# Decoder kernel on one core: products made for other head pairs placed at other steps of a pair, and the doubled-key copies issued one and two steps later

## The chip, the cores and the metric

The kernel runs on one core of a Trainium2 chip. Its engines run their own instruction queues in order and wait for one another through semaphores: TensorE (PE, matrix products), VectorE (DVE), ScalarE (ACT), GpSimd (POOL), and SyncE (SP), which here issues nearly all DMAs. The metric is the device time in microseconds (us) of the whole program.

## The reference

Four batch rows of 1024 tokens of width 256 pass through six sublayers, each `x = x + f(layernorm(x))`: a kernel attention, a cross attention to 64 context rows, one expert of eight, a causal self attention with 16 heads of width 64, a second cross attention, and a gated feed-forward with quantised weights. The change lies in the self attention:

```python
q = jnp.einsum('bsd,hqd->bhsq', x, w_q)
k = jnp.einsum('bsd,hqd->bhsq', x, w_k)
v = jnp.einsum('bsd,hvd->bhsv', x, w_v)
scores = jnp.einsum('bhsq,bhtq->bhst', q, k)
masked = jnp.where(causal, -jnp.inf, scores)
weights = jax.nn.softmax(masked / jnp.sqrt(jnp.float32(dq)), axis=-1)
out = jnp.einsum('bhst,bhtv->bhsv', weights, v)
return jnp.einsum('bsf,df->bsd', cat, w_o)
```

## The kernel before

The four batch rows are done one after the other. In the self attention the 16 heads are 8 **pairs** j = 0 to 7, and a pair is 16 **blocks** k = 0 to 15: head 0, then head 1, each with its eight tiles of 128 query rows. The tiles come in the order 7, 0, 6, 1, 5, 2, 4, 3, and tile i has (i+1)*128 causal columns, so a block of even k is wide (1024, 896, 768, 640 columns) and one of odd k narrow (128 to 512). g = 16*j + k numbers the 128 blocks of a batch row. One block passes through these stations:

- PE `l_score`: scores into PSUM (lines 1271 to 1273, the last with `causal`). Wide blocks have two pairs of banks in turn, narrow ones all share bank 4.
- DVE `l_max`: row maximum `nmax` (line 1385). ACT `l_exp`: exponentials to `l_pb` (wide) or `l_ps` (narrow), line 1336. POOL: high half in f16 to `l_phb`/`l_phs` (line 1494). DVE `l_lower`: the remainder (line 1391), called the **remainder of block g** below.
- SP `l_flip`: one transposing DMA to `l_ptb`/`l_pts` (line 1503), called **flip g**. It waits for the remainder.
- PE `l_pv`: probabilities times values (line 1289), called **pv g**; it waits for flip g to land. DVE `l_finish` divides every fourth block (lines 1398, 1403).

All engines walk through the blocks in **steps** g in code order. At step g PE issues the scores of block g+6 (AHEAD = 6), then a task if the step has one, then pv g. ACT issues the exponential of block g+5 and then its part of the task. DVE issues the maximum of block g+6, its part of the task, the remainder of block g+4, and each fourth step a finish. SP issues flip g+4 and then copies or loads that are set for this step.

A **task** is a product made for another pair; `l_tasks(j, k)` says which task stands at which step. K0, K1, Q0, Q1 are the halves of the keys and queries of pair j+1 (6 matmuls of 512 columns, lines 233 to 235). V0 to V3 are the values for the next two pairs (in pairs 1, 3, 5). T0, T1 turn the output of pair j-1 (line 1225). O0 to O3 are the output projection of two done pairs (line 1250, in pairs 2, 4, 6). All tasks of the loop use PSUM bank 5, so `l_pe` makes a task wait until the bank's last reader of the task before it has run:

```python
before = in_bank5[in_bank5.index(t) - 1]
if before[0] == "T":
    pe.wait_ge(*upper(b, before))
else:
    pe.wait_ge(*lower(b, before))
```

"Upper" is ACT's part of a task (K: line 1347 into `xn`; Q: line 1351, two operations; T: line 1363), "lower" is DVE's, which waits for upper (K: line 1440, Q: line 1444, two operations each; O: line 1412 alone, without ACT). Pair 7 has tasks of its own (`CONTEXT`), which are not touched.

The keys are needed twice on 128 partitions. SP's `l_dup(j, h)` copies them for head h of pair j, two DMAs (line 1511), called **dup0** and **dup1**. `l_score` has the first block of a pair (k = 0, issued by PE at step 10 of the pair before) wait for the lower part of Q1 and for dup0, and block k = 8 for dup1:

```python
if i == NT - 1:
    pe.wait_ge(*lower(b, ("Q", j, 1)))
    pe.wait_ge(q_[f"dup{h}"], (b * HP + j + 1) * 32)
```

Of the kernel before, what the change touches and what calls it, by code (L numbers as in the profile page):

```python
# [19 lines left out]
HP = 8  # L20
# [37 lines left out]
def decoder_kernel(nc, a, out):  # L58
    ctx = ExitStack()
    with ctx:  # L60
# [1063 lines left out]
        q_ = l_sem  # L1124
# [11 lines left out]
        def l_tasks(j, k):  # L1136


            if j == HP - 1 and k in CONTEXT:
                return CONTEXT[k]  # L1140
            if k in (0, 1):
                return ("K", j + 1, k) if j + 1 < HP else None
            if k in (2, 3):
                return ("T", j - 1, k - 2) if j >= 1 else None
            if k in (4, 5):
                return ("Q", j + 1, k - 4) if j + 1 < HP else None
            if k in (7, 9, 11, 13):
                if j % 2 == 0 and j >= 2:
                    return "O", j // 2 - 1, (k - 7) // 2
                if j % 2 == 1 and j + 1 < HP:  # L1150
                    return "V", (j + 1) // 2, (k - 7) // 2
            return None

        FIRST_BANK = {("K", 0, 0): 2, ("K", 0, 1): 3, ("Q", 0, 0): 4, ("Q", 0, 1): 7,
# [10 lines left out]
        def made(b, t):  # L1165
            return q_["made"], b * len(N_MADE) + N_MADE[t]
# [4 lines left out]
        def lower(b, t):  # L1171
            return q_["lower"], b * len(N_LOWER) + N_LOWER[t]
# [233 lines left out]
        def l_make_lower(v, b, t):  # L1406
# [7 lines left out]
            if kind == "C":  # L1414
                v.wait_ge(*made(b, t))
                for c in range(2):
                    v.tensor_scalar(X1["c_kT"][:, c, :], bank[:, c * CK:(c + 1) * CK], x1_bk[:, c:c + 1], None, ALU.add)
                    v.tensor_scalar(X1["c_vT"][:, c, :], bank[:, (2 + c) * CK:(3 + c) * CK], x1_bv[:, c:c + 1], None, ALU.add)
                v.drain()
                for src, dst in ((X1["c_kT"], l_kC), (X1["c_vT"], X1["c_vC"])):  # L1420
                    for c in range(2):
                        last = v.tensor_tensor(dst[:, c, :].rearrange("p (h k) -> p h k", k=CK), src[:, c, :].unsqueeze(1).to_broadcast([P, 8, CK]),
                                               blk1[:].unsqueeze(2).to_broadcast([P, 8, CK]), ALU.mult)
                last.then_inc(q_["lower"], 1)
                return
# [96 lines left out]
        def l_sp(sp, b):  # L1522
            sp.wait_ge(s_xu, b * (NPH * NT) + 2 * NT)
            for j in range(2):
                l_load_w(sp, b, j)
            l_load_wv(sp, b, 0)
            l_load_wo(sp, b, 0)
            for h in range(2):
                l_dup(sp, b, 0, h)
            for g in range(4):  # L1530
                l_flip(sp, b, g)
            for g in range(NB):
                j, k = g // NB1, g % NB1
                if g + 4 < NB:
                    l_flip(sp, b, g + 4)
                if j + 1 < HP and k == 4:
                    l_dup(sp, b, j + 1, 0)
                if j + 1 < HP and k == 10:
                    l_dup(sp, b, j + 1, 1)
                if j + 2 < HP and k == 2:  # L1540
                    sp.wait_ge(*lower(b, ("Q", j + 1 - 1, 1)))
                    l_load_w(sp, b, j + 2)
                if j % 2 == 0 and j + 2 < HP and k == 2:
                    sp.wait_ge(*lower(b, ("V", j // 2, 3)))
                    l_load_wv(sp, b, j // 2 + 1)
                if j % 2 == 1 and j >= 3 and k == 2:
                    sp.wait_ge(*lower(b, ("O", j // 2 - 1, 3)))
                    l_load_wo(sp, b, j // 2)
# [549 lines left out]
```

## Time and profile before

| | |
|---|---|
| median of 3 runs | 3018.18 us (3016.68 to 3021.74) |
| the profiled execution, its own time | 3010.78 us |
| span of its trace | 3008.8 us |
| mean granted TensorE clock | 0.867 of full speed |
| busy: PE / DVE / ACT / POOL | 2276.8 / 2175.1 / 1060.2 / 585.9 us |
| self attention, four times | about 340, 335, 338 and 335 us |

The span is the part of the profiled execution between its first and last instruction. An engine's busy time counts neither its waits nor, for SP, the issuing of DMAs; a share under 100% in a stretch is time in which the engine waited for another. In a timeline, "[x <-E n]" behind a row is the idle time before it and what ended that idle time.

### The profile page before, as it was taken

The numbers are of one execution on the slowest core, as the hardware profiler recorded it, in microseconds if no ns is written. First come the engines' busy times: TensorE is split into PE (matmuls) and PEld (weight loads), VectorE is DVE, ScalarE is ACT, GpSimd is POOL, SyncE is SP. The second block draws the span as 40 slices with busy tenths as digits, with TensorE's granted clock in tenths as the row PEclk, the third lists the DMA queues.
The fourth block names the chain that finished last, engine by engine and source line by source line (L and its number), as shares of the span: only waits on it lengthen the run. The fifth ranks groups of instructions, "written<-read, shape, count | busy, mean of one in ns | idle before, by whom it ended". The sixth has DMA issues, their size and how long they took to land.

```text
span 3008.8 us, 50636 instructions
## 1 busy us (share of the span) xinstructions
PE 2276.8 (76%) x17470; PEld 1830.6 (61%) x17470; DVE 2175.1 (72%) x4246; ACT 1060.2 (35%) x2004; POOL 585.9 (19%) x666
## 2 busy tenths in 40 slices
PE   3667788868776877886877687888677777888875
PEld 3556666657465756664755565666565566666663
DVE  6765788866866578885776667888586666788767
ACT  2312444422432244442242224444224223444324
POOL 2111222212101122221101112222120102222220
PEclk8778899989777889998877789999877878999988
DMA  6001689840001078983000119897100014899600
GB/s 234 1 15 40 137 160 171 154 86 1 1 15 56 15 149 161 170 152 63 1 1 15 56 37 167 166 164 144 31 1 15 1 55 85 161 169 166 113 1 14
DMA packets 658407, 251.39 MB, mean 84 GB/s; under 512 B 613082, under 2 KB 633946, under 8 KB 657370
## 3 DMA queue, kind: packets, MB, share of 16 engines
q1 hardware_dynamic: 653978, 243.79, 41.4%
q10 hardware_dynamic: 4160, 4.19, 0.4%
q8 instruction: 146, 2.39, 0.3%
q14 instruction: 123, 1.01, 0.1%
HBM read 52.87 MB, written 10.49 MB: 21 GB/s over the span
## 4 chain that ended last, share of the span: by engine, by line
issue 38%; PE 23%; DVE 18%; DMA 11%; ACT 5%; POOL 4%; DVEq 1%; ACTq 0%; SPq 0%; POOLq 0%
DMA l_ptb<-l_phb 6%; PE ps L233 5%; PE ps L235 5%; PE ps L234 4%; DMA l_pts<-l_phs 4%; DVE nmax L1385 3%; PE ps L1289 1%; DVE l_k L1440 1%; DVE l_q L1444 1%; DVE l_phb L1391 1%; DVE l_phs L1391 1%; ACT l_q L1351 1%; PE ps L1271 1%; ACT xn L1347 1%; POOL d_pn L990 1%
## 5 line engine op out<-in xcount | busy, mean ns | idle before, releaser
L1385 DVE TENSOR_REDUCE nmax<-ps 128x1 f32<-128x1024 f32 (+7 forms) x512 | 383.3, 750 | 23.0 <-PE ps L1273 20.9
L1494 POOL CAST l_phb<-l_pb 128x1024 f16<-128x1024 f32 (+3 forms) x256 | 241.4, 943 | 654.1 <-ACT l_pb L1336 337.8
L1336 ACT ACTIVATE l_pb<-ps,nmax 128x1024 f32<-128x1024 f32 (+3 forms) x256 | 244.7, 956 | 283.5 <-DVE nmax L1385 282.7
L1271 PE MATMUL ps<-l_k,l_q 128*128 128x512 f32 (+3 forms) x768 | 319.1, 416 | 24.3 <-ACT l_ps L1336 23.9
L1391 DVE TENSOR_TENSOR l_phb<-l_pb,l_phb 128x1024 f16<-128x1024 f32 (+3 forms) x256 | 288.2, 1126 | 15.5 <-POOL l_phb L1494 13.4
L1272 PE MATMUL ps<-l_k,l_q 128*128 128x512 f32 (+3 forms) x768 | 270.1, 363 | 0.0
L1289 PE MATMUL ps<-l_v,l_ptb 128*128 128x64 f16 x4992 | 197.8, 197 | 34.2 <-DMA l_ptb<-l_phb 34.1
L1289 PEld LDWEIGHTS ps<-l_v,l_ptb 128*128 128x128 f16 x4992 | 177.1, 101 | 67.4 <-DMA l_ptb<-l_phb 41.1
L233 PE MATMUL ps<-xTh,l_w 128*128 128x512 f32 x256 | 123.1, 481 | 83.9 <-DVE l_q L1444 50.5
L1494 POOL CAST l_phs<-l_ps 128x128 f16<-128x128 f32 (+3 forms) x256 | 124.2, 485 | 319.1 <-DMA l_pts<-l_phs 169.6
L1271 PEld LDWEIGHTS ps<-l_k,l_q 128*128 128x128 f32 x768 | 156.0, 203 | 44.2 <-ACT l_ps L1336 29.8
L1336 ACT ACTIVATE l_ps<-ps,nmax 128x128 f32<-128x128 f32 (+3 forms) x256 | 135.5, 529 | 107.6 <-DVE nmax L1385 106.4
L1272 PEld LDWEIGHTS ps<-l_k,l_q 128*128 128x128 f32 x768 | 157.1, 205 | 12.6
L1289 PE MATMUL ps<-l_v,l_pts 128*128 128x64 f16 x1920 | 105.6, 200 | 62.1 <-DMA l_pts<-l_phs 61.8
L1391 DVE TENSOR_TENSOR l_phs<-l_ps,l_phs 128x128 f16<-128x128 f32 (+3 forms) x256 | 134.3, 525 | 25.1 <-POOL l_phs L1494 23.1
L303 PE MATMUL ps<-idf,xn 128*128 128x128 f32 x320 | 66.0, 374 | 108.0 <-DVE xTl L322 68.0
L1289 PEld LDWEIGHTS ps<-l_v,l_pts 128*128 128x128 f16 x1920 | 84.1, 102 | 104.1 <-DMA l_pts<-l_phs 68.7
L316 ACT CAST xTh<-ps 128x512 fp32r<-128x512 f32 x80 | 45.5, 587 | 285.7 <-PE ps L303 285.7
L985 POOL TENSOR_TENSOR x<-x,x_bo 128x2048 f32<-128x2048 f32 x8 | 36.2, 4521 | 553.7 <-DVE xn L284 553.7
L1440 DVE TENSOR_TENSOR l_k<-ps,xn 64x512 fp32r<-64x512 f32 x128 | 88.1, 689 | 73.1 <-ACT xn L1347 71.4
L1444 DVE SCALAR_TENSOR_TENSOR l_q<-ps,l_q 64x512 fp32r<-64x512 f32 x128 | 88.2, 689 | 68.8 <-ACT l_q L1351 66.6
L303 PEld LDWEIGHTS ps<-idf,xn 128*128 128x128 f32 x320 | 53.1, 195 | 117.9 <-DVE xTl L322 55.5
(361 smaller groups left out, 6279.4 us busy)
## 6 DMA issues: line engine op xcount, KB each, us to landing
l_k<-xn SPq DMA_DIRECT2D x128, 256.0 KB, 4.1
l_w<-l_wqk_s SPq DMA_DIRECT2D x32, 512.0 KB, 4.8
l_wv<-l_wv_s SPq DMA_DIRECT2D x16, 512.0 KB, 6.0
xin<-in_x SPq DMA_DIRECT2D x4, 1024.0 KB, 5.5
m_w<-in_m_w SPq DMA_DIRECT2D x8, 512.0 KB, 4.4
m_w<-in_m_w SPq DMA_DIRECT2D x4, 1024.0 KB, 9.2
l_wo<-in_l_wo SPq DMA_DIRECT2D x16, 256.0 KB, 4.5
l_ptb<-l_phb SPq DMA_TRANSPOSE x256, 4.1
```

Of the source, the lines that this page charges most:

```text
L233: pe.matmul(o, lh, rh, start=start, stop=False)
L234: pe.matmul(o, lh, rl, start=False, stop=False)
L235: return pe.matmul(o, ll, rh, start=False, stop=stop)
L303: last = pe.transpose(o, xn[:, tile, c * P:(c + 1) * P], idf[:])
L1271: pe.matmul(s[:, c0:c1], q, L["l_k1"][:, h, c0:c1], start=True, stop=False)
L1272: pe.matmul(s[:, c0:c1], q, L["l_k2"][:, j % 2, h, c0:c1], start=False, stop=c1 < n)
L1289: last = pe.matmul(o, l_turned(k)[:, pp * (i + 1) + m, :], L["l_v"][:, (j // 2) % 2, vv, m, cols], start=m == 0 and n == 0, stop=m == i an ...
L1336: s.activation(l_numer(k)[:, 0:n], l_banks(k)[:, 0:n], ACT.Exp, bias=nmax[:, k % 4:k % 4 + 1], accum_out=lsum[:, h, k % NT:k % NT + 1]).th ...
L1385: v.tensor_reduce(nmax[:, k % 4:k % 4 + 1], l_banks(k)[:, 0:n], AX.X, ALU.max, negate=True).then_inc(q_["max"], 1)
L1391: v.tensor_tensor(l_parts(k)[:, n:2 * n], l_numer(k)[:, 0:n], l_parts(k)[:, 0:n], ALU.subtract).then_inc(q_["lo"], 1)
L1444: last = v.scalar_tensor_tensor(out=L["l_q"][other, n % 2, h, halves(g)], in0=bank[mine, :], scalar=0.125, in1=f32(L["l_q"][mine, n % 2, h ...
L1494: g.tensor_copy(l_parts(k)[:, 0:cols], l_numer(k)[:, 0:cols]).then_inc(q_["hi"], 1)
```

## The change

Within a pair, K1 goes from step 1 to 4, Q0 and Q1 from 4 and 5 to 6 and 8, and V0 to V3 or O0 to O3 from steps 7, 9, 11, 13 to 10, 12, 14, 15. K0 (step 0) and T0, T1 (steps 2, 3) stay. SP issues dup0 at step 6 for 4 and dup1 at step 11 for 10. In pair 7 the lower part of the task C gets a wait for the last dup1, since it writes over the buffer that the copy reads.

```diff
-            if k in (0, 1):
-                return ("K", j + 1, k) if j + 1 < HP else None
+            if k in (0, 4):
+                return ("K", j + 1, k // 4) if j + 1 < HP else None
             if k in (2, 3):
                 return ("T", j - 1, k - 2) if j >= 1 else None
-            if k in (4, 5):
-                return ("Q", j + 1, k - 4) if j + 1 < HP else None
-            if k in (7, 9, 11, 13):
+            if k in (6, 8):
+                return ("Q", j + 1, k // 2 - 3) if j + 1 < HP else None
+            if k in (10, 12, 14, 15):
                 if j % 2 == 0 and j >= 2:
-                    return "O", j // 2 - 1, (k - 7) // 2
+                    return "O", j // 2 - 1, (10, 12, 14, 15).index(k)
                 if j % 2 == 1 and j + 1 < HP:
-                    return "V", (j + 1) // 2, (k - 7) // 2
+                    return "V", (j + 1) // 2, (10, 12, 14, 15).index(k)
...
                 v.drain()
+                v.wait_ge(q_["dup1"], (b * HP + HP) * 32)
...
-                if j + 1 < HP and k == 4:
+                if j + 1 < HP and k == 6:
                     l_dup(sp, b, j + 1, 0)
-                if j + 1 < HP and k == 10:
+                if j + 1 < HP and k == 11:
                     l_dup(sp, b, j + 1, 1)
```

Three places show what this does to the queues. First SP in pair 1, from flip 8 on (`128x16x128` is a flip of 1024 columns in two halves; `l_k<-xn` is half a dup). Before:

```order
L1503 DMA_TRANSPOSE l_ptb<-l_phb 128x16x128 [waits l_pv,l_lo]
L1511 DMA l_k<-xn 64x1024 [waits l_score,l_upper]
L1511 DMA l_k<-xn 64x1024
L1503 DMA_TRANSPOSE l_pts<-l_phs 128x2x128 [waits l_pv,l_lo]
L1503 DMA_TRANSPOSE l_ptb<-l_phb 128x14x128 [waits l_pv,l_lo]
L1503 DMA_TRANSPOSE l_pts<-l_phs 128x4x128 [waits l_pv,l_lo]
L1503 DMA_TRANSPOSE l_ptb<-l_phb 128x12x128 [waits l_pv,l_lo]
L1503 DMA_TRANSPOSE l_pts<-l_phs 128x6x128 [waits l_pv,l_lo]
L1503 DMA_TRANSPOSE l_ptb<-l_phb 128x10x128 [waits l_pv,l_lo]
L1511 DMA l_k<-xn 64x1024 [waits l_score,l_upper]
L1511 DMA l_k<-xn 64x1024
L1503 DMA_TRANSPOSE l_pts<-l_phs 128x8x128 [waits l_pv,l_lo]
```

After:

```order
L1504 DMA_TRANSPOSE l_ptb<-l_phb 128x16x128 [waits l_pv,l_lo]
L1504 DMA_TRANSPOSE l_pts<-l_phs 128x2x128 [waits l_pv,l_lo]
L1504 DMA_TRANSPOSE l_ptb<-l_phb 128x14x128 [waits l_pv,l_lo]
L1512 DMA l_k<-xn 64x1024 [waits l_score,l_upper]
L1512 DMA l_k<-xn 64x1024
L1504 DMA_TRANSPOSE l_pts<-l_phs 128x4x128 [waits l_pv,l_lo]
L1504 DMA_TRANSPOSE l_ptb<-l_phb 128x12x128 [waits l_pv,l_lo]
L1504 DMA_TRANSPOSE l_pts<-l_phs 128x6x128 [waits l_pv,l_lo]
L1504 DMA_TRANSPOSE l_ptb<-l_phb 128x10x128 [waits l_pv,l_lo]
L1504 DMA_TRANSPOSE l_pts<-l_phs 128x8x128 [waits l_pv,l_lo]
L1512 DMA l_k<-xn 64x1024 [waits l_score,l_upper]
L1512 DMA l_k<-xn 64x1024
```

Dup0 stood right behind flip 8 and now stands behind flips 9 and 10; dup1 stood between flips 14 and 15 and now stands behind flip 15.

Second DVE in pair 2, steps 4 to 6: from the finish of step 4 (line 1403) to the remainder of block 10 (`l_phb` 128x896), on which flip 10 waits. `nmax` rows are maxima. Before:

```order
L1399 REGISTER_ALU
L1402 REGISTER_ALU [waits l_pv,l_rc]
L1403 TENSOR_TENSOR xn<-ps,recs 128x4x64 [waits l_made]
L1384 REGISTER_ALU
L1385 TENSOR_REDUCE nmax<-ps 128x1 [waits l_score]
L1426 REGISTER_ALU
L1444 SCALAR_TENSOR_TENSOR l_q<-ps,l_q 64x512 [waits l_upper]
L1444 SCALAR_TENSOR_TENSOR l_q<-ps,l_q 64x512
L1391 TENSOR_TENSOR l_phs<-l_ps,l_phs 128x128 [waits l_hi]
L1384 REGISTER_ALU
L1385 TENSOR_REDUCE nmax<-ps 128x1 [waits l_score]
L1391 TENSOR_TENSOR l_phb<-l_pb,l_phb 128x896 [waits l_hi]
```

After (line numbers behind the added line are one higher):

```order
L1399 REGISTER_ALU
L1402 REGISTER_ALU [waits l_pv,l_rc]
L1403 TENSOR_TENSOR xn<-ps,recs 128x4x64 [waits l_made]
L1384 REGISTER_ALU
L1385 TENSOR_REDUCE nmax<-ps 128x1 [waits l_score]
L1391 TENSOR_TENSOR l_phs<-l_ps,l_phs 128x128 [waits l_hi]
L1384 REGISTER_ALU
L1385 TENSOR_REDUCE nmax<-ps 128x1 [waits l_score]
L1427 REGISTER_ALU
L1445 SCALAR_TENSOR_TENSOR l_q<-ps,l_q 64x512 [waits l_upper]
L1445 SCALAR_TENSOR_TENSOR l_q<-ps,l_q 64x512
L1391 TENSOR_TENSOR l_phb<-l_pb,l_phb 128x896 [waits l_hi]
```

The lower part of a query task now stands right ahead of the remainder of block 10, with both maxima ahead of it. Just above each piece stands the task of step 4, Q0 before and K1 after.

Third PE in pair 2, up to the first score of pair 3 (step 10). Before, from the scores of block 15 (step 9) on:

```order
L1263 REGISTER_ALU
L1271 MATMUL ps<-l_k,l_q 128x512 [waits l_exp]
L1272 MATMUL ps<-l_k,l_q 128x512
L1273 MATMUL ps<-causal,idb 128x128
L1308 REGISTER_ALU
L1250 MATMUL ps<-l_wo,xin 128x256 [waits l_lower]
L1250 MATMUL ps<-l_wo,xin 128x256 x3
L1289 MATMUL ps<-l_v,l_pts 128x64 [waits l_pt1]
L1289 MATMUL ps<-l_v,l_pts 128x64 x2
L1259 ISA [waits l_lower]
L1261 REGISTER_ALU [waits l_dup0]
L1271 MATMUL ps<-l_k,l_q 128x512 [waits l_exp]
```

After, from pv 8 on (the six matmuls of Q1 stand right above):

```order
L1282 ISA [waits l_o]
L1289 MATMUL ps<-l_v,l_ptb 128x64 [waits l_pt0]
L1289 MATMUL ps<-l_v,l_ptb 128x64 x23
L1263 REGISTER_ALU
L1271 MATMUL ps<-l_k,l_q 128x512 [waits l_exp]
L1272 MATMUL ps<-l_k,l_q 128x512
L1273 MATMUL ps<-causal,idb 128x128
L1289 MATMUL ps<-l_v,l_pts 128x64 [waits l_pt1]
L1289 MATMUL ps<-l_v,l_pts 128x64 x2
L1258 REGISTER_ALU
L1259 ISA [waits l_lower]
L1261 REGISTER_ALU [waits l_dup0]
```

The two waits, `l_lower` for Q1 and `l_dup0`, stand in the same place. Between Q1 and them stood the scores of blocks 12 to 15, pv 5 to 9 and two O tasks; now there are pv 8, the scores of block 15 and pv 9.

## Rows read from the trace of the kernel before

**Rows 1.** The page's first part: busy us of each engine.
```profile
PE 2276.8 (76%) x17470; PEld 1830.6 (61%) x17470; DVE 2175.1 (72%) x4246; ACT 1060.2 (35%) x2004; POOL 585.9 (19%) x666
```

**Rows 2.** Windows: the four self attentions summed (length, busy PE, PEld, DVE, ACT, POOL).
```profile
sum 1348.00, PE 1081.19 PEld 852.26 DVE 1074.87 ACT 601.26 POOL 359.47; mean PE 270.30 PEld 213.06 DVE 268.72 ACT 150.32 POOL 89.87
```

**Rows 3.** Waits of PE over the span: us in total, times, longest.
```profile
PE ps L1289 <- DMA l_pts<-l_phs: 61.8, 38, 3.9
PE ps L233 <- DVE l_q L1444: 50.9, 31, 1.9
PE ps L1289 <- DMA l_ptb<-l_phb: 34.1, 48, 1.9
...
PE ps L1225 <- DVE l_k L1440: 23.7, 24, 1.2
...
PE ps L233 <- DVE l_k L1440: 16.9, 22, 0.9
```

**Rows 4.** Timeline of PE, pair 4 of the last batch row: start, us.
```profile
2689.75 0.23 PE L1273 MATMUL ps<-causal,idb 128*128 128x128 bf16 x1
...
2697.29 0.66 PE L1225 MATMUL ps<-idf,xn 128*128 128x128 f32 x4 [0.93 <-DVE l_k L1440]
...
2700.85 0.50 PE L233 MATMUL ps<-xTh,l_w 128*128 128x512 f32 x1 [0.38 <-ACT xin L1363]
...
2705.23 0.50 PE L233 MATMUL ps<-xTh,l_w 128*128 128x512 f32 x1 [1.78 <-DVE l_q L1444]
...
2713.88 1.95 PE L1250 MATMUL ps<-l_wo,xin 128*128 128x256 f32 x8
...
2715.75 0.47 PE L1271 MATMUL ps<-l_k,l_q 128*128 128x512 f32 x1
...
2718.72 0.79 PE L1289 MATMUL ps<-l_v,l_ptb 128*128 128x64 f16 x21 [1.74 <-DMA l_ptb<-l_phb]
...
2728.34 0.52 PE L1289 MATMUL ps<-l_v,l_pts 128*128 128x64 f16 x12 [0.84 <-DMA l_pts<-l_phs]
...
2729.42 0.23 PE L1273 MATMUL ps<-causal,idb 128*128 128x128 bf16 x1
```

**Rows 5.** Timeline of SP, same pair: flip 8, dup0, flip 10.
```profile
2707.18 1.90 SPq L1503 DMA_TRANSPOSE l_ptb<-l_phb  x1
2709.17 1.60 SPq L1511 DMA_DIRECT2D l_k<-xn  x2
...
2712.95 1.38 SPq L1503 DMA_TRANSPOSE l_ptb<-l_phb  x1
```

**Rows 6.** Timeline of DVE, same pair.
```profile
2697.86 1.23 DVE L1385 TENSOR_REDUCE nmax<-ps 128x1 f32<-128x1024 f32 x1
...
2703.78 1.39 DVE L1444 SCALAR_TENSOR_TENSOR l_q<-ps,l_q 64x512 fp32r<-64x512 f32 x2 [2.17 <-ACT l_q L1351]
2705.21 1.94 DVE L1391 TENSOR_TENSOR l_phb<-l_pb,l_phb 128x1024 f16<-128x1024 f32 x1
...
2707.61 0.41 DVE L1385 TENSOR_REDUCE nmax<-ps 128x1 f32<-128x256 f32 x1
...
2710.77 1.08 DVE L1391 TENSOR_TENSOR l_phb<-l_pb,l_phb 128x896 f16<-128x896 f32 x1
```

**Rows 7.** Timeline of ACT, same pair: exponential 8, upper part of Q0, exponential 11.
```profile
2699.12 1.12 ACT L1336 ACTIVATE l_pb<-ps,nmax 128x1024 f32<-128x1024 f32 x1 [0.55 <-DVE nmax L1385]
...
2702.56 1.20 ACT L1351 ACTIVATE l_q<-ps 64x512 fp32r<-64x512 f32 x2 [1.39 <-PE ps L235]
...
2708.14 0.47 ACT L1336 ACTIVATE l_ps<-ps,nmax 128x256 f32<-128x256 f32 x1
```

**Rows 8.** Line 1511 (dup0 and dup1) in the first self attention: issue to landing.
```profile
DMA to landing us min/median/max: 3.0/4.1/5.3
```

**Rows 9.** Windows in the first self attention; the clock is the 0.50.
```profile
502.60:506.00 3.40, 3.40 (x31) 3.00 (x31) 3.06 (x8) 1.75 (x4) 0.00 (x0) 0.50 1.07 114
```

**Rows 10.** Timeline of PE, pair 0 of the last batch row, pv 15.
```profile
2566.42 0.52 PE L1289 MATMUL ps<-l_v,l_pts 128*128 128x64 f16 x12 [2.38 <-DMA l_pts<-l_phs]
```

## The prediction

> **What bounds the kernel now.** I read the page first, then the self attention by windows, then the waits of PE, then one pair in the timelines. Only the self attention is touched, 1348 of the 3008.8 us of the span [rows 2]. There PE is busy 1081 us (80%) and DVE 1075 us (80%) [rows 2], a share close to that of the whole program [rows 1], and neither is full. The reader should see two engines that hand one another work and each wait for about a fifth of the time. So nothing is bought by work alone, since no work is removed; only waits can go or come.
>
> The waits of PE that end within the pairs are of two kinds [rows 3]. Tasks that stand too close in bank 5: PE waits for the lower part of a query task 50.9 us, for that of a key task 23.7 us (before T0) and 16.9 us (before K1). And flips that land late: 61.8 us for narrow blocks, 34.1 us for wide ones. The sample pair shows where: T0 waits 0.93, Q0 0.38 for T1, Q1 1.78, pv 10 1.74 and pv 15 0.84 us [rows 4]. This pair takes from 2689.98 (end of the scores of block 6) to 2729.65, so 39.67 us [rows 4]. Seven such periods, pair 0 to pair 6, make up most of one self attention, 28 in the program.
>
> **What the change removes.** K1 no longer follows K0, T0 no longer follows K1, Q1 no longer follows Q0. Counting all that rows 3 list, 91.5 us of waits lose their cause, about 3.3 us a period. The spread also puts O or V tasks over steps 10 to 15, where pv 10 and pv 15 wait for flips. A task there adds work but covers such a wait.
>
> **What it adds.** Three of the four query and key tasks move towards the end of a chain that has a fixed end, the first scores of the next pair at step 10. They need the lower part of Q1 and dup0. I follow this chain through the sample pair, with durations from its rows.
>
> K1 at step 4. Maximum 8 on DVE starts at 2697.86, and exponential 8 1.26 us later [rows 6, 7]; 1.73 us after that exponential's start the task of step 4 starts, at 2700.85 [rows 4, 7], since it waits for ACT's part of T1. Without the lower part of K1 at step 1 (two operations, as long as the 1.39 us of a query's [rows 6]) maximum 8 starts near 2696.4, so K1 starts near 2699.4.
>
> Lower part of K1. The upper part of Q0 started 1.71 us after its first matmul [rows 4, 7]. For K1 that is 2701.1. It is one ACT operation where Q0's 1.20 us are two [rows 7], so 0.6 us. DVE then has 2701.7 to 2703.1. Remainder 8 takes 1.94 us [rows 6]; with the finish behind it, maximum 11 starts 2.40 us after remainder 8 (2705.21 to 2707.61 [rows 6]), here at 2705.5, and ends at 2705.9.
>
> Lower part of Q0, now at step 6. ACT has exponential 11 ahead of it (0.47 us and some 0.2 to read the sum, taken as 0.7 [rows 7]): 2706.6. Upper part 1.20, to 2707.8; lower part 1.39, to 2709.2; remainder 10 1.08, to 2710.3 [rows 6, 7]. Before, it ended at 2711.85 [rows 6]. So up to here the new order is 1.5 us ahead.
>
> Dup0. Before, it was issued at 2709.17, behind flip 8 [rows 5]. Now it stands behind flip 10, which waits for remainder 10. Flip 10 holds SP 1.38 us, to 2711.7, and the second half of dup0 is issued 0.8 us later (two take 1.60) [rows 5], at 2712.5. From issue to landing takes 3.0 to 5.3 us, median 4.1 [rows 8]; with 4.0 it lands at **2716.5**. The first scores of the next pair stood at 2715.75 [rows 4] and did not wait for dup0. They do now, and start 0.75 us later. PE has by then done Q1, pv 8, the scores of block 15 and pv 9 near 2712.4, and idles some 4 us: the removed waits come back in one piece, behind SP and a DMA.
>
> The rule of the Trainium skill that bears on this is in "DMA: Bandwidth & Descriptors", section "Queues, rings and completion order": each DMA engine takes descriptors in ring order. By it a copy issued behind three flips sits behind their data. The spread of rows 8, 3.0 to 5.3 us, agrees with such a queue; the sum above uses about the median, and a landing at the upper end would make it worse.
>
> From those scores to the end of the pair. Before: 2715.75 to 2729.65, 13.9 us, with 1.74 and 0.84 us of waits for flips in it [rows 4], so 11.3 us of PE's own. The new order has two more O or V tasks here. An O task takes 1.8 us (2713.88 to 2715.75 less the three matmuls of pv 9 [rows 4]); a V task has as many columns as a query task, whose first matmul stood 1.71 us before ACT's part [rows 4, 7], so I take 1.5 us, and 0.2 us for V3 waiting on V2, an estimate between nothing and the 0.7 us by which 16.9 us over 22 waits made K1 wait for K0 [rows 3]. The waits for flips are gone, since PE's standstill let SP and the DMAs catch up. So 2.58 us of waits go and two tasks come: 3.6 us in pairs 2, 4, 6 (+1.0 us), 3.2 us in pairs 1, 3, 5 (+0.6 us). With the 0.75 us the period grows by 1.75 or 1.35 us. Over 24 such periods, with a mean of 1.5: **+36 us**.
>
> Pair 0 has neither T nor O nor V tasks. Its K1 need not wait for T1, and its wait at pv 15, 2.38 us in the last batch row [rows 10], goes, since dup1 no longer stands ahead of flip 15. I take 3 us each, **-12 us** for four.
>
> Costed at nothing: dup1 one step later, which block 8 of the next pair needs seven steps on; the added wait of task C for dup1, five steps behind its issue (uncovered it would cost at most the 4 us of a landing, four times 16 us); the loads of weights, which keep their steps.
>
> **Sum:** 3010.78 + 36 - 12 = 3035 us for the profiled execution. That one lay 7.4 us under the median of the runs, so 3042 us for the median.
>
> **The rivals.** *Faster: dup0 lands in time.* The sum turns at about 1 us: if dup0 lands by 2715.5, the 24 periods lose only what pair 0 gives. For it speak that remainder 8 at 1.94 us may be a drawn-out one (remainder 10 with 7/8 of the columns takes 1.08 [rows 6]), and that landings go down to 3.0 us [rows 8]. Then the lower part of Q1 decides: Q1 is made from 2709.2, its upper part waits for exponential 13, and its lower part ends near 2714.3. The period is 0.4 us shorter with O and 0.8 with V tasks: -15 us, with pair 0 -27 us, so 2991 us; with a short remainder 8 another 0.7 us each, 2974 us.
>
> *Much slower: the clock.* At 502.6, right after a wait of PE of 1.8 us, the granted clock was 0.50, that is 1.2 instead of 2.4 GHz, for 3.4 us, with PE busy throughout [rows 9]. A standstill of 4 us in each pair may bring such a stretch each time. It does the work of 1.7 us: +41 us over 24 periods, 3083 us. Against it: the waits that used to be elsewhere caused such stretches too. The Trainium skill, "TensorE: Matmul & The Clock Gate", section "HAM oscillation", says that a wait for a DMA in every turn of a loop re-throttles each turn; by that this rival would be the outcome.
>
> *Slower: the ring.* Dup0 lands 5.3 us after issue each time [rows 8]: +1.3 us in 24 periods, 31 us, 3073 us.
>
> *No change:* waits only move. The 3.3 us removed and the flips covered are just balanced by the standstill, 3012 to 3024 us.
>
> **How the numbers follow.** Forecast as summed, 3025 to 3060 us: 0.35. Clock: 0.15. Ring: 0.10. No change: 0.10. Faster: 0.30. About 6 us, 0.2%, is what the measurement can tell from no change. Slower by more than that 0.60, within it 0.10, faster 0.30. The range runs from between the two faster results, 2980, to just short of the clock's, 3080.
>
> **What the new profile would show.** Right: no waits of PE for `l_q` of 1.8 us before line 233; a wait of about 4 us before the first scores of a pair (line 1271), ended by the DMA `l_k<-xn`; waits for `l_pts` and `l_ptb` much shorter; dup0 issued right behind flip 10; DVE's lower part of Q0 right ahead of remainder 10. Wrong: if the wait at step 10 is ended by DVE's lower part of Q1, dup0 was early and the time falls. If flips 12 to 15 still make PE wait, the covering failed and it is slower than I say. If the granted clock in the self attentions falls under what it was, the clock has a part.

## The result and the profile after

The changed kernel takes 3098.23 us (median of 4 runs, 3089.28 to 3107.17) against 3017.43 us (4 runs, 3011.69 to 3021.74) before: a ratio of 1.0269, interval 1.0233 to 1.0305. So it is slower by 81 us, where the forecast said 25 us slower, and it lies above the range. The profiled execution took 3107.17 us with a span of 3105.1 us and a mean granted clock of 0.850 (before: 0.867).

The first part of the page, as [rows 1]:

```profile
PE 2325.4 (75%) x17470; PEld 1870.1 (60%) x17470; DVE 2177.3 (70%) x4246; ACT 1053.9 (34%) x2004; POOL 602.1 (19%) x666
```

The counts are the same. DVE's busy time is 2.2 us more, but PE's has grown by 49 us with not one matmul more: the same work took longer, as it does at a lower clock.

The windows over the seven periods from pair 0 to pair 6 in each batch row, with the sum of the four (length, busy PE, PEld, DVE, ACT, POOL, then the clock). Before:

```profile
319.70:606.20 286.50, 233.51 (x2418) 186.59 (x2418) 232.66 (x359) 128.35 (x292) 77.07 (x112) 0.94 0.88 161
...
sum 1135.80, PE 923.57 PEld 738.52 DVE 930.45 ACT 513.19 POOL 309.41; mean PE 230.89 PEld 184.63 DVE 232.61 ACT 128.30 POOL 77.35
```

After:

```profile
323.80:631.80 308.00, 244.59 (x2418) 194.78 (x2418) 232.97 (x360) 126.62 (x292) 79.77 (x112) 0.90 0.82 150
...
sum 1224.60, PE 971.92 PEld 774.11 DVE 931.94 ACT 506.32 POOL 325.71; mean PE 242.98 PEld 193.53 DVE 232.99 ACT 126.58 POOL 81.43
```

These 28 periods hold 88.8 of the 96.3 us by which the span grew: 48 us of it is PE's longer busy time, the rest waits.

The waits of PE that answer to [rows 3]:

```profile
PE ps L1271 <- DMA l_k<-xn: 94.7, 21, 5.1
...
PE ps L1271 <- ACT l_ps L1336: 59.6, 48, 2.1
PE ps L1225 <- DVE xn L1403: 43.2, 28, 3.0
PE ps L1271 <- issue: 31.8, 7, 4.9
```

The waits for flips and for `l_q` before line 233 are no longer among the longest. In their place stand the first scores of the next pair: 21 times put down to dup0 and 7 times to "issue", 28 in all, with 94.7 + 31.8 = 126.5 us, 4.5 us each. The standstill of "some 4 us" is there in every pair. Within the 28 periods the waits for flips fell from 95.7 to 19.0 us, and those before line 233 for `l_q` from 50.5 to 11.8. The wait before T0 (line 1225) did not go. It changed its cause, from 23.7 us for the lower part of K1 to 24.9 us for DVE's finish (`xn`, line 1403); and the waits of scores for ACT's exponential of a narrow block (`l_ps`, line 1336) grew from 12.1 to 46.6 us.

The same pair as in [rows 4], pair 4 of the last batch row, from 2767.35 (end of the scores of block 6) to 2812.02, so 44.67 us for 39.67 before. PE:

```profile
2786.41 0.50 PE L233 MATMUL ps<-xTh,l_w 128*128 128x512 f32 x1 [0.64 <-DVE l_q L1445]
...
2789.46 0.25 PE L1289 MATMUL ps<-l_v,l_pts 128*128 128x64 f16 x3
2794.36 0.76 PE L1271 MATMUL ps<-l_k,l_q 128*128 128x512 f32 x1 [4.65 <-issue]
2794.93 0.63 PE L1272 MATMUL ps<-l_k,l_q 128*128 128x512 f32 x1
```

Dup0 of this pair landed at 2794.27, 0.09 us before the first scores start, though the row says "issue". SP, as [rows 5]:

```profile
2787.50 1.52 SPq L1504 DMA_TRANSPOSE l_ptb<-l_phb  x1
2789.11 1.70 SPq L1512 DMA_DIRECT2D l_k<-xn  x2
```

And the windows of this stretch (the clock stands behind the count of POOL):

```profile
2786.00:2789.50 3.50, 3.06 (x35) 2.21 (x36) 3.11 (x5) 1.39 (x4) 1.70 (x2) 1.00 0.36 72
2789.50:2794.30 4.80, 0.21 (x5) 0.09 (x3) 3.91 (x7) 2.01 (x5) 1.21 (x2) 0.95 1.02 198
2794.30:2801.20 6.90, 6.84 (x39) 5.25 (x40) 2.33 (x3) 1.20 (x2) 1.65 (x2) 0.54 0.77 88
2801.20:2806.00 4.80, 4.80 (x55) 4.11 (x52) 4.00 (x6) 1.56 (x4) 1.07 (x2) 1.00 0.72 136
```

Read the second row: PE stands still, and near its end the clock falls. In the third PE is busy without a break, at 0.54: the matmul of 512 columns takes 0.63 to 0.76 us where it takes 0.40 to 0.50 at full clock. Before, the first scores followed at full clock, without a wait [rows 4]. In 23 of the 28 periods of the changed kernel a stretch at 1.2 GHz begins in this standstill, 6.8 us long each time, and in 4 more one of 3.4 us begins within 1.2 us behind its end.

The table compares all kernels in the same way: from the end of the scores of block 6 of a pair (step 0) to the same point of the next, over all four batch rows. "Half clock" is the time at 1.2 GHz in one period. "Dup0 landed" (its second half) and "first scores" (their end) are counted from the start of the period, and "rest" is from the end of the first scores to the end of the period. "PE idle" is PE's time in waits. Medians are of the whole program; the other columns are means over pairs 1 to 6 of the four batch rows (and pair 0 in its own column), worked out from the traces, in us.

| kernel | median | pair 0 | pairs 1 to 6 | PE idle | half clock | dup0 landed | first scores | rest |
|---|---|---|---|---|---|---|---|---|
| before | 3017.43 | 40.73 | 40.54 | 7.0 | 2.50 | 25.25 | 27.91 | 12.63 |
| after | 3098.23 | 39.18 | 44.49 | 8.7 | 7.54 | 27.45 | 29.65 | 14.84 |
| dup0 at step 4 | 2980.95 | 36.27 | 39.75 | 5.8 | 1.85 | 22.88 | 25.96 | 13.79 |
| dup0 at step 5 | 2983.90 | 36.32 | 39.78 | 5.9 | 1.90 | 24.15 | 25.95 | 13.83 |
| tasks only | 2995.14 | 40.45 | 39.77 | 5.6 | 2.54 | 22.75 | 26.02 | 13.75 |
| copies only | 3112.09 | 39.35 | 44.65 | 9.4 | 7.25 | 31.82 | 33.86 | 10.79 |
| dup1 only | 2997.80 | 36.73 | 40.64 | 7.0 | 3.13 | 27.11 | 29.67 | 10.98 |
| unused products | 3056.63 | 39.67 | 42.69 | 5.1 | 1.21 | 27.74 | 29.15 | 13.54 |
| V and O only | 3061.27 | 40.69 | 42.70 | 7.3 | 6.48 | 25.22 | 28.12 | 14.58 |
| V and O, unused products | 3051.80 | 41.38 | 41.72 | 5.3 | 0.96 | 24.84 | 27.84 | 13.88 |
| K and Q only | 3078.57 | 40.37 | 43.56 | 8.1 | 6.24 | 23.15 | 31.39 | 12.17 |
| dup0 from ACT | 3096.08 | 40.43 | 44.06 | 9.6 | 6.68 | 22.28 | 30.53 | 13.53 |
| all earlier | 2977.90 | 36.77 | 39.56 | 5.3 | 3.70 | 23.10 | 25.53 | 14.03 |
| all earlier, spread | 2968.06 | 36.00 | 39.35 | 5.9 | 1.99 | 23.20 | 25.81 | 13.55 |

### The profile page after: what moved, and what is told of

The parts are those of the page before. It is cut to its first block, busy times and chain, and to the rows that moved or that the text cites. A ratio compares the mean times of both kernels' runs of the same rounds, so it can differ in the third digit from the quotient of the medians.

```text
span 3105.1 us, 50639 instructions
## 1 busy us (share of the span) xinstructions
PE 2325.4 (75%) x17470; PEld 1870.1 (60%) x17470; DVE 2177.3 (70%) x4246; ACT 1053.9 (34%) x2004; POOL 602.1 (19%) x666
## 4 chain that ended last, share of the span: by engine, by line
issue 37%; PE 28%; DVE 19%; ACT 5%; DMA 5%; POOL 3%; DVEq 1%; SPq 1%; POOLq 0%; ACTq 0%
PE ps L233 5%; DVE l_phb L1391 4%; PE ps L234 4%; PE ps L235 4%; PE ps L1250 3%; DVE nmax L1385 3%; DMA l_k<-xn 3%; PE ps L1271 3%; PE ps L1289 2%; PE ps L1272 2%; ACT l_q L1351 2%; DVE l_k L1441 1%; DVE l_phs L1391 1%; POOL x L985 1%; POOL d_pn L990 1%
## 5 line engine op out<-in xcount | busy, mean ns | idle before, releaser
L1271 PE MATMUL ps<-l_k,l_q 128*128 128x512 f32 (+3 forms) x768 | 325.3, 424 | 189.4 <-DMA l_k<-xn 94.7
L1495 POOL CAST l_phb<-l_pb 128x1024 f16<-128x1024 f32 (+3 forms) x256 | 257.1, 1004 | 750.6 <-DMA l_ptb<-l_phb 437.7
L1272 PE MATMUL ps<-l_k,l_q 128*128 128x512 f32 (+3 forms) x768 | 276.6, 372 | 0.0
L233 PE MATMUL ps<-xTh,l_w 128*128 128x512 f32 x256 | 124.6, 487 | 30.2 <-DVE l_q L1445 11.8
L1391 DVE TENSOR_TENSOR l_phs<-l_ps,l_phs 128x128 f16<-128x128 f32 (+3 forms) x256 | 142.0, 555 | 0.3 <-POOL l_phs L1495 0.3
L1273 PE MATMUL ps<-causal,idb 128*128 128x128 bf16 x512 | 123.8, 242 | 0.0
L1250 PE MATMUL ps<-l_wo,xin 128*128 128x256 f32 x384 | 111.2, 440 | 0.7 <-DVE x L1412 0.5
```

Source lines behind the costliest of these rows:

```text
L233: pe.matmul(o, lh, rh, start=start, stop=False)
L1250: last = pe.matmul(bank[:, u * D:(u + 1) * D], l_oT[:, m, tok], L["l_wo"][:, m, :], start=m == 0, stop=m == 1)
L1271: pe.matmul(s[:, c0:c1], q, L["l_k1"][:, h, c0:c1], start=True, stop=False)
L1272: pe.matmul(s[:, c0:c1], q, L["l_k2"][:, j % 2, h, c0:c1], start=False, stop=c1 < n)
L1273: pe.matmul(s[:, n - P:n], idb[:], causal[:], start=False, stop=True).then_inc(q_["score"], 1)
L1391: v.tensor_tensor(l_parts(k)[:, n:2 * n], l_numer(k)[:, 0:n], l_parts(k)[:, 0:n], ALU.subtract).then_inc(q_["lo"], 1)
```

## The experiments

**The theory:** the new times of the tasks are good, and nearly all that is lost comes from dup0 at step 6: it lands after PE has run out of work, and the standstill both costs time and leaves PE at half clock behind it. **The rivals:** the tasks themselves are what costs (two more behind the first scores), or the ring makes all late copies slow.

**Dup0 alone put back.** The changed kernel with one number different:

```diff
-                if j + 1 < HP and k == 6:
+                if j + 1 < HP and k == 4:
                     l_dup(sp, b, j + 1, 0)
```

> The changed kernel with dup0 issued at step 4 again, behind flip 8; all else as changed. Theory A (dup0 stands too late in SP's queue, PE stands still some 5 us before the first scores of each pair and its clock falls): in the changed kernel dup0 landed 27.45 us into a pair and the lower part of Q1 ended at 24.51, so the scores start near 24.6, PE's standstill shrinks from about 4.7 to 1.5 us and the half-clock stretches go; 4 to 4.6 us less in 28 periods, 2970 to 3000 us. Theory B (the places of the tasks cost the time: V or O tasks at 14 and 15, query tasks near the pair's end): 3070 to 3100 us, as the changed kernel.

Measured: 2980.95 us (2978.74 to 2983.72), ratio to before 0.9879 (0.984 to 0.9918). One copy, two steps earlier, is worth 117 us, and the kernel is now faster than before. Its waits of PE no longer have a row for `l_k<-xn`:

```profile
PE ps L1271 <- ACT l_ps L1336: 56.5, 45, 2.1
PE ps L1225 <- DVE xn L1403: 42.2, 29, 3.0
PE ps L1289 <- DMA l_pts<-l_phs: 34.8, 39, 2.5
...
PE ps L1271 <- DVE l_q L1445: 21.2, 22, 1.5
```

The first scores now wait for the lower part of Q1, for about a microsecond (21.2 us in 22 times), which is the case "dup0 lands in time" of the prediction. The time, too, is within what that rival gave, 2974 to 2991 us.

**The copies alone.** The kernel before with dup0 at step 6, dup1 at step 11 and the wait of C:

```diff
-                if j + 1 < HP and k == 4:
+                if j + 1 < HP and k == 6:
                     l_dup(sp, b, j + 1, 0)
-                if j + 1 < HP and k == 10:
+                if j + 1 < HP and k == 11:
                     l_dup(sp, b, j + 1, 1)
```

> The kernel before with the two copies alone moved (dup0 at step 6, dup1 at step 11), tasks where they were. Theory A: dup0 lands behind flip 10, near 29.4 us of a pair instead of 25.3, against scores that wanted to start at 26.8; a standstill of 2.6 us more and a fallen clock (up to 1.7 us) in 28 periods, 3090 to 3140 us. Theory B: the copies are no matter, 3010 to 3030 us.

Measured: 3112.09 us (3107.18 to 3115.41), ratio 1.0306 (1.0264 to 1.0348). Two copies moved in SP's queue, and no product, make the kernel 3% slower, more than the whole change does.

```profile
PE ps L1271 <- DMA l_k<-xn: 73.2, 21, 4.9
...
PE ps L1289 <- DMA l_ptb<-l_phb: 66.4, 40, 3.5
PE ps L233 <- DVE l_q L1445: 50.6, 29, 1.9
```

It has the old waits, such as the one before Q1, and the new one as well.

**Dup1 alone,** at step 11 in the kernel before, with the wait of C:

```diff
-                if j + 1 < HP and k == 10:
+                if j + 1 < HP and k == 11:
                     l_dup(sp, b, j + 1, 1)
```

> The kernel before with dup1 alone moved from step 10 to 11. With the tasks moved, dup1 at 11 against 10 gave 2981 against 2995 us, all of it in pair 0 (36.3 against 40.5 us). Theory A: here too pair 0 no longer waits at pv 15 behind dup1 and loses 3 to 4 us in each of four batch rows, the other pairs up to 0.5 us: 2995 to 3010 us. If it only helps with the tasks moved: 3012 to 3022 us.

Measured: 2997.80 us (9 runs, 2993.25 to 3006.11), ratio 0.9939 (0.992 to 0.9958). The gain is in pair 0: 40.73 to 36.73 us, while pairs 1 to 6 stand. The 2.38 us of pv 15 [rows 10] are gone in that place, and with them what followed. In pairs 1 to 6 the wait only moved: the rest of the period is 1.7 us shorter (12.63 to 10.98), but the first scores come 1.8 us later in it (27.91 to 29.67), and where PE waited 61.8 us for narrow flips and 34.1 for wide ones [rows 3], it is now the wide ones:

```profile
PE ps L1289 <- DMA l_ptb<-l_phb: 83.9, 59, 3.6
...
PE ps L1289 <- DMA l_pts<-l_phs: 12.8, 11, 3.0
```

The kernel with both copies moved differs from this one in dup0 alone, and takes 114 us more: all of its loss is dup0's. The wait that C got costs nothing that shows.

**The tasks alone:** the changed kernel with both copies at their old steps, 4 and 10.

```diff
-                if j + 1 < HP and k == 6:
+                if j + 1 < HP and k == 4:
                     l_dup(sp, b, j + 1, 0)
-                if j + 1 < HP and k == 11:
+                if j + 1 < HP and k == 10:
                     l_dup(sp, b, j + 1, 1)
```

> The changed kernel with both copies where they stood before, dup0 at step 4 and dup1 at 10: the move of the tasks alone. Theory A: dup1 one step earlier matters little, 2970 to 3000 us, beside 2981 with dup1 at 11. Its rival: dup1 between flips 14 and 15 again makes pv 15 wait, above all in pair 0, where 2 to 3 us of wait came back (4 to 12 us in all) and 1 us in the others, 2990 to 3015 us.

Measured: 2995.14 us (10 runs, 2991.36 to 3010.11), ratio 0.9942 (0.9922 to 0.9961). Pairs 1 to 6 take 39.77 us, as with dup0 at step 4 and dup1 at 11, but pair 0 takes 40.45 us instead of 36.27. Pair 0 of the last batch row shows why. Dup1 again stands ahead of flip 15, and in this row PE comes out of the wait at half clock (12 products of 64 columns in 0.82 us, 0.52 before [rows 10]):

```profile
2549.76 0.82 PE L1289 MATMUL ps<-l_v,l_pts 128*128 128x64 f16 x12 [2.51 <-DMA l_pts<-l_phs]
```

These runs give the parts of the change. A pair of 1 to 6: tasks -0.77, dup1 -0.02, dup0 +4.74 us. Pair 0: tasks -0.28, dup1 -4.18, dup0 +2.91 us. (Each is the difference of two rows of the table: tasks only to before, dup0 at step 4 to tasks only, after to dup0 at step 4.)

**Dup0 one step later than in the kernel before,** at step 5 of the changed kernel, which puts it behind flip 9 and ahead of flip 10:

```diff
-                if j + 1 < HP and k == 6:
+                if j + 1 < HP and k == 5:
                     l_dup(sp, b, j + 1, 0)
```

> The changed kernel with dup0 issued at step 5, behind flip 9, between the 4 of the run that gave 2981 us and the 6 of the changed kernel. Theory A: flip 9 is issued at 17.85 us of a pair and ends at 19.2, so dup0 lands near 24.6 (22.9 with step 4, 27.5 with step 6), almost when the lower part of Q1 ends (24.5); the standstill stays near 1.5 us and the clock mostly up, 2980 to 3005 us. If SP's order were not the matter, but any move of dup0 behind the task of step 4: as the changed kernel, 3080 to 3100 us.

Measured: 2983.90 us (2971.62 to 2985.95), ratio 0.9885 (0.9845 to 0.9925). Dup0 lands 1.27 us later than from step 4, at 24.15 us, and the first scores end at 25.95 us, as from step 4 (25.96): the lower part of Q1, which ends at 24.4, covers it. All of the loss lies between steps 5 and 6, that is in standing behind flip 10, whose remainder comes behind the lower part of Q0.

**Is it the wait or the clock behind it?** The changed kernel, with 18 unused products of 512 columns ahead of the wait of the first scores, in pairs 1 to 7 (the loop is the added work; its results are written over):

```diff
             if i == NT - 1:
+                if h == 0 and j >= 1:
+                    if g >= 4:
+                        pe.wait_ge(q_["exp"], b * NB + g - 3)
+                    for _ in range(18):
+                        pe.matmul(l_banks(k)[:, 0:HALF], L["l_q"][:, (j - 1) % 2, h, 0:P], L["l_k2"][:, (j - 1) % 2, h, 0:HALF], start=True, stop=True)
                 pe.wait_ge(*lower(b, ("Q", j, 1)))
```

> The changed kernel with 18 matmuls of 512 columns added ahead of the first scores of pairs 1 to 7, before the waits for Q1's lower part and for dup0; they write the PSUM banks that the scores overwrite, and their results are not used. They take about 4 us at the full clock, inside the standstill of about 5 us. Theory A with the clock as its second half: the granted clock stays at 2.4 GHz through the standstill, the work behind it is 1.5 to 2 us shorter in 28 periods, 3040 to 3060 us. If the fallen clock costs nothing (the loss is the wait alone): 3095 to 3115 us. If the wait isn't there: some 100 us slower, 3200 us.

Measured: 3056.63 us (3055.85 to 3070.96), ratio 1.0142 (1.0095 to 1.0188), 42 us less than the changed kernel, for more work. PE of the same pair, where the standstill was (lines are five higher):

```profile
2751.21 0.25 PE L1294 MATMUL ps<-l_v,l_pts 128*128 128x64 f16 x3
2751.29 4.35 PE L1262 MATMUL ps<-l_k,l_q 128*128 128x512 f32 x18
2755.48 0.39 PE L1276 MATMUL ps<-l_k,l_q 128*128 128x512 f32 x1
2755.71 0.39 PE L1277 MATMUL ps<-l_k,l_q 128*128 128x512 f32 x1
```

The first scores stand at full clock, and the windows show 0.97 where they showed 0.90:

```profile
322.10:617.10 295.00, 257.58 (x2545) 205.79 (x2544) 233.51 (x359) 126.86 (x292) 86.41 (x112) 0.97 0.86 156
```

Dup0 lands no earlier (27.74 us), so the copy's lateness is untouched; what went is half clock, 7.54 to 1.21 us in a period. The clock's share of the loss is thus about 1.8 us a pair (44.49 to 42.69), and 2.1 us (42.69 against 40.54 before) are left for the rest. Of the 1.8 us, 1.3 lie behind the first scores (the rest of the period, 14.84 to 13.54) and 0.5 ahead of their end.

**V and O alone** moved, in the kernel before, to see what the two more tasks behind the first scores cost:

```diff
-            if k in (7, 9, 11, 13):
+            if k in (10, 12, 14, 15):
```

> The kernel before with V0 to V3 and O0 to O3 alone moved to steps 10, 12, 14, 15; K, Q and both copies as before. Theory A: two tasks fewer ahead of the next pair's first scores let them start as soon as dup0 lands (25.3 instead of 26.8 us of a pair), and the late tasks cover 2.4 us of waits for flips with 3.2 of work: 0.5 to 0.9 us less in 24 periods, 2990 to 3010 us. Theory B: the late V or O tasks cost the time, 3040 us or more.

Measured: 3061.27 us (3050.91 to 3071.23), ratio 1.0131 (1.0087 to 1.0174). A miss of 50 us, in the sign too. No wait for dup0 is in it; the half clock is, 6.48 us a period. The same pair, PE in steps 8 and 9:

```profile
2760.44 0.86 PE L1289 MATMUL ps<-l_v,l_ptb 128*128 128x64 f16 x24 [1.10 <-DMA l_ptb<-l_phb]
2761.84 0.50 PE L1271 MATMUL ps<-l_k,l_q 128*128 128x512 f32 x1 [0.54 <-ACT l_ps L1336]
...
2763.41 0.34 PE L1289 MATMUL ps<-l_v,l_pts 128*128 128x64 f16 x3 [0.77 <-DMA l_pts<-l_phs]
2763.57 0.78 PE L1271 MATMUL ps<-l_k,l_q 128*128 128x512 f32 x1
```

and its windows:

```profile
2756.60:2763.50 6.90, 4.17 (x66) 3.17 (x66) 6.69 (x10) 3.23 (x9) 1.23 (x2) 0.98 0.94 183
2763.50:2766.90 3.40, 3.40 (x12) 2.48 (x13) 2.78 (x6) 0.93 (x4) 1.42 (x3) 0.54 0.88 170
```

The kernel before, at about the same place of the period:

```profile
2707.00:2713.90 6.90, 6.44 (x82) 5.24 (x78) 6.66 (x13) 3.34 (x8) 1.23 (x2) 1.00 0.94 184
```

Steps 6 to 9 have lost both their tasks, DVE is nearly full there as it was before (6.69 and 6.66 of 6.90 us), and PE was busy 4.17 of those 6.90 us in pieces, with no wait over 1.10 us; then the clock fell. In the kernel before PE was busy 6.44 of 6.90 us there and the clock was full. So the clock also falls without one long stop. The Trainium skill has this in "TensorE: Matmul & The Clock Gate", section "A second HAM failure mode: psum-queue depth-cycling": in another kernel, small idle times between groups of matmuls came often enough to make the clock swing. This trace agrees, with the 0.54 behind waits of 1.10, 0.54 and 0.77 us.

**The same with unused products:** 8 ahead of the scores of blocks 13 and 15 each.

```diff
+            if k in (13, 15) and j >= 1:
+                for _ in range(8):
+                    pe.matmul(s[:, 0:HALF], L["l_q"][:, j % 2, h, 0:P], L["l_k2"][:, j % 2, h, 0:HALF], start=True, stop=True)
```

> The kernel with only V and O moved (3061 us; half clock in 6.8 us of a pair, where the kernel before has 3.0, most of it around the next pair's first scores) with 8 matmuls of 512 columns whose results are not used ahead of the scores of blocks 13 and 15, where two of the V or O tasks stood before. Theory C (the steps 6 to 9, emptied of tasks, leave PE idle so much that its clock falls just when the work of steps 10 to 12 begins): the half clock goes back to 3 us a pair, and the period is 1 to 2 us shorter in 24 periods in spite of 3.7 us more of work, 3015 to 3040 us. If the clock has nothing to do with it: 3060 to 3100 us.

Measured: 3051.80 us (3045.73 to 3055.70), ratio 1.0114 (1.0079 to 1.0149). The half clock goes, 6.48 to 0.96 us, and so do 2.0 us of idle time, but the gain is 10 us and not the 21 to 46 that the expectation came to. The 16 products are 3.7 us of work a pair at 0.23 us each (the 18 above took 4.35 us with the pipeline's end). Of these 3.7 us only 2.0 went into idle time and the rest adds to PE's work; in the run above they filled a standstill. (The expectation counts half clock as 6.8 and 3.0 us; by the table it is 6.48 and 2.50.) So the half clock of the kernel with V and O moved comes from PE's lack of work in steps 6 to 9, which is shown; what it costs there is not shown by itself, since filling the steps with unused products trades one loss for another.

**K and Q alone:** V and O at their old steps, the copies too.

```diff
-            if k in (10, 12, 14, 15):
+            if k in (7, 9, 11, 13):
```

> The changed kernel with V and O at steps 7, 9, 11, 13 as before and both copies at steps 4 and 10 as before: K1, Q0 and Q1 alone moved. Theory A: the waits of K1, T0 and Q1 go (3.3 us a pair), but now the task of step 9 waits for the lower part of Q1 (24.5 us of a pair) and takes 1.8 us ahead of the first scores, which start near 26.4, as before at 26.8; 0 to 0.8 us less in 28 periods, 2995 to 3017 us. If the moved K and Q tasks alone made the gain of the run with 2981 us: 2975 to 2990 us.

Measured: 3078.57 us (3075.63 to 3080.73), ratio 1.0197 (1.0159 to 1.0234). A miss of 60 us, and dup0 lands early (23.15 us). The waits of PE:

```profile
PE ps L1271 <- ACT l_ps L1336: 70.0, 65, 2.1
...
PE ps L233 <- DVE l_q L1445: 39.0, 25, 1.8
PE ps L1250 <- DVE l_q L1445: 38.3, 24, 1.8
```

The tasks at steps 6, 7, 8 and 9 stand one behind the other in bank 5. V tasks in pairs 1, 3, 5 (line 233) and O tasks in pairs 2, 4, 6 (line 1250) wait for `l_q`, some 24 times each, so twice a pair: at step 7 for the lower part of Q0, at step 9 for that of Q1. Q1 slips, its lower part ends at 28.3 us of the period instead of 24.5, and the first scores end at 31.39. So neither half of the moves is good alone: the task list works only as a whole.

**Dup0 past SP.** The changed kernel with dup0 issued from ACT's queue, behind the upper part of K1, on which it waits anyway:

```diff
                 if t and t[0] not in "OC":
                     l_make_upper(s, b, t)
+                if t and t[0] == "K" and t[2] == 1:
+                    l_dup(s, b, t[1], 0)
...
-                if j + 1 < HP and k == 6:
-                    l_dup(sp, b, j + 1, 0)
```

> The changed kernel with dup0 issued by ACT right behind its upper part of K1 (step 4), from ACT's own DMA queue, and none on SP. Theory A (SP's queue order makes dup0 late, the data are there long before): the copy lands near 18 us of a pair, the lower part of Q1 at 24.5 alone decides, SP is 1.8 us freer in its busiest stretch; as with step 4 or a little less, 2955 to 2985 us. If the copy's data or the DMA rings were what makes it late: 3050 to 3100 us.

Measured: 3096.08 us (3071.59 to 3104.05), ratio 1.0241 (1.0187 to 1.0295). A miss of over 100 us. For the copies of ACT over the whole program:

```profile
DMA to landing us min/median/max: 3.0/9.4/13.2
```

For all copies in the changed kernel's first self attention, issued by SP, as [rows 8]:

```profile
DMA to landing us min/median/max: 3.1/4.0/4.7
```

ACT, then SP, then PE of the kernel with the copy on ACT, in the same pair:

```profile
2782.08 1.31 ACTq L1514 DMA_DIRECT2D l_k<-xn  x2
```

```profile
2781.58 1.94 SPq L1506 DMA_TRANSPOSE l_pts<-l_phs  x1
2784.76 8.35 SPq L1506 DMA_TRANSPOSE l_ptb<-l_phb  x1
2793.20 1.20 SPq L1506 DMA_TRANSPOSE l_pts<-l_phs  x1
```

```profile
2793.95 0.82 PE L1289 MATMUL ps<-l_v,l_pts 128*128 128x64 f16 x12 [7.01 <-DMA l_pts<-l_phs]
```

The copy is issued at about 12 us of a period, where SP issued it at about 22. Flip 8, which comes next, held SP 8.35 us instead of the usual 1.5. Pv 7 waited 7.01 us for flip 7, which had been issued ahead of the copy. The second queue did not pass the first, it held it up. The copy itself still landed at 22.28 us of a period on the mean, before the lower part of Q1, which now ended at 29.03; it is the flips it held up that made the first scores late.

The Trainium skill, "DMA: Bandwidth & Descriptors", section "Queues, rings and completion order", has each DMA engine take turns between the queues that have work. The trace agrees in this: from 2787 to 2791 ACT's queue moved 0.27 MB and SP's 0.10 MB. But the DMA engines, busy all that time, moved 94 GB/s together, and 192 GB/s from 2793 to 2797, when SP's queue was alone. Why the rate falls, no run here tells.

**All tasks of K, T and Q one step earlier where they can be,** with dup0 at step 4 and dup1 at 11: K at 0, 2; T at 3, 4; Q at 5, 7; V and O at 10, 12, 14, 15; pair 7 unchanged.

```diff
-            if k in (0, 4):
+            if k in (0, 2):
...
-            if k in (2, 3):
+            if k in (3, 4):
...
-            if k in (6, 8):
+            if k in (5, 7):
```

> A new order on the same theory: K0, K1 at 0 and 2, T0, T1 at 3 and 4, Q0, Q1 at 5 and 7, V or O at 10, 12, 14, 15, dup0 at 4, dup1 at 11; pair 7 as before. Theory A (the first scores of the next pair must come early and PE must not stand idle): the lower part of Q1 ends some 1.5 us earlier than 24.5 us of a pair, T0 no longer waits 1 us for the finish; period 38.5 to 39.5 instead of 39.75 us in 24 pairs: 2950 to 2975 us. Rival: with steps 8 and 9 free of tasks PE's clock falls as when V and O alone were moved, 2990 to 3040 us.

Measured: 2977.90 us (2975.86 to 2981.61), ratio 0.9865 (0.9828 to 0.9902), just over what was expected. The idle time, 5.3 us, is the least of all kernels without unused products, but half clock is up at 3.70 us, from 1.85 with dup0 at step 4.

**The same with V and O at 9, 11, 13, 14,** so that steps 8 and 9 are not without a task:

```diff
-            if k in (10, 12, 14, 15):
+            if k in (9, 11, 13, 14):
```

> As the order with K1 at 2 and Q1 at 7, but V or O at 9, 11, 13, 14. If the clock is what an idle stretch ahead of step 10 costs: better than the same with 10, 12, 14, 15, 2945 to 2970 us. If the first scores' start decides: one task ahead of them makes them 1 to 1.8 us later and nothing is gained, 2965 to 3000 us.

Measured: 2968.06 us (2960.53 to 2973.89), ratio 0.9833 (0.9792 to 0.9874), the fastest of all: 49 us under the kernel before and 130 us under the changed one. The windows:

```profile
324.50:602.00 277.50, 229.26 (x2419) 183.99 (x2418) 231.98 (x358) 127.15 (x290) 79.05 (x112) 0.96 0.90 166
...
sum 1088.60, PE 912.93 PEld 730.83 DVE 925.22 ACT 509.69 POOL 319.09; mean PE 228.23 PEld 182.71 DVE 231.31 ACT 127.42 POOL 79.77
```

PE's busy time, 912.9 us, is 59 us under the changed kernel's, for the same matmuls. Half clock is down to 1.99 us. DVE is busy 925 of these 1089 us (85%) and PE 913 (84%).

## Why the prediction was right in kind and wrong in size

**What stood.** The chain to the standstill came nearly as it was worked out. Flip 10 started at 20.42 us of a period on the mean (forecast 2710.3, which is 20.3 after 2689.98); the lower part of Q1 ended at 24.51 (forecast 24.3). The waits before Q1 and most of those for flips went, the standstill stood before line 1271 and was 4.5 us (forecast some 4), and dup0 decided the sign. The wait before T0 did not go: the prediction saw that T0 no longer follows K1, and not that DVE's finish would then hold it as long (24.9 us for 23.7). This did not enter the sum, which went by the chain to dup0. The rival "dup0 lands in time" is borne out as well: with dup0 at step 4 or 5 the time was 2981 and 2984 us.

**What failed** is the step that made the fallen clock a rival with a chance of 0.15, and so put the clock at nothing in the sum, beside a forecast which itself contained a standstill of 4 us. The two were not two cases: the standstill was there in all 28 periods, and half clock began in it or within 1.2 us behind it in 27 of them. It cost about 1.8 us a pair, as the run with unused products shows; the forecast had 0. [Rows 9] had shown it behind a wait of 1.8 us, and the argument against ("the waits that used to be elsewhere caused such stretches too") was weighed without a count. The count is: 2.50 us of half clock in a period of pairs 1 to 6 before, 7.54 after. The rule of the Trainium skill that the rival named, "TensorE: Matmul & The Clock Gate", section "HAM oscillation", a wait for a DMA in each turn of a loop throttling each turn, was the outcome here; with it in the sum the forecast would have been that rival's 3083 us.

**The terms,** a pair of 1 to 6:

| term | forecast | measured |
|---|---|---|
| first scores later, at full clock | +0.75 | +0.92 |
| these scores themselves at half clock | 0 | +0.82 |
| two more tasks less the waits for flips | +0.75 | +0.9 |
| the tasks behind, at half clock | 0 | +1.3 |
| sum | +1.5 | +3.95 |

The first: dup0 landed at 27.45 us, and where the clock was full behind such a landing (the runs with copies only and with unused products) the first scores ended 1.38 us behind it, so 28.83, for 27.91 before. The second: they ended at 29.65. The landing itself was forecast for 26.5; it came 0.95 us later, since the second half of dup0 was issued at 23.15 instead of 22.5 (flip 10 took 1.47 us and the first half of dup0 held SP 1.1 us, where 1.38 and 0.8 were assumed) and landed 4.3 instead of 4.0 us on. The term still came out nearly right, because the sample pair was 0.9 us ahead of the mean in the kernel before: two errors that cancel, by luck. The last two: the rest of the period grew by 2.21 us, and half clock in it from 0.33 to 3.00 us. Half of that difference is 1.3 us, and 1.3 us is also what the unused products gave back in the rest (14.84 to 13.54); 0.9 us are left for the tasks. The two clock terms are 2.1 us together; the run with unused products gained 1.8, since its dup0 landed 0.3 us later.

**Pair 0** gained 1.55 us and not 3. Dup1 behind flip 15 gives 4.18 us there, more than was thought, but dup0 costs 2.91, which the prediction left out: it had no term for the new wait in pair 0.

**The sum** for the profiled execution: 24 periods at 3.95 are 95 us (36 forecast), pair 0 is -6 (-12 forecast), and 7.6 us lie outside the 28 periods. That is the 96.4 us between the two profiled executions. The one of the changed kernel was its slowest run, 9 us over the median; what the 7.6 us are is open.

**Costed at nothing, and rightly:** dup1's step for later pairs (-0.02 us in sum; alone, it moved a wait from one place of the period to another) and the wait of C (the kernel with both in it is faster than before). The rival "the ring" did not come: landings stayed at 3.1 to 4.7 us with a median of 4.0 in the first self attention ([rows 8]: 3.0, 4.1, 5.3), and dup0's second half took 4.3 us on the mean in both kernels, behind one flip and behind three. The copy was late because it was issued late.

**What is open:** why a plain copy from a second queue and transposes of the first slow each other, what the late V or O tasks cost without the clock, and how the clock's fall depends on what PE did; the runs show only where it fell and what stood ahead.

## What to carry to other kernels

A small copy on a serial queue costs what the instruction that it stands behind waits for: look at the queue's neighbour (here flip 10, behind a DVE remainder, behind a query's lower part), and not at the step's number, since step 5 was free and step 6 cost 4.7 us a pair. When a forecast itself contains a standstill of PE, put the clock that comes after it into the sum, at half speed for the next microseconds of work, and look in the windows of the kernel before for how short a wait has already brought it. When tasks are spread anew, look at the steps that they leave as well as those that they go to: steps with none let the clock fall though no wait was long.

## What the hardware showed that was not expected

- Two copies moved by one and two places in a queue cost 3% of a program of 3 ms, with every task where it was (ratio 1.0306).
- The clock fell behind a stretch of 6.90 us in which PE was busy 4.17 us and its longest wait was 1.10 us; 18 unused products a pair, 4.35 us of work, made the changed kernel 42 us faster.
- Plain copies from ACT's queue beside transposes on SP's took 9.4 us from issue to landing (median, up to 13.2) where SP's take 4.0, and one transpose held SP 8.35 us; with both queues at work the DMA engines moved 94 GB/s, with SP's alone 192.
